# Cross attention and routed experts on one core: expert rows read as quarters and turned in 32x32 squares on VectorE, residual rows fetched by plain transfers

## What is computed

```python
x = x + attention(layernorm(x), ctx, ctx)      # 16 heads of 32, masks, Wq Wk Wv Wo
idx = argmax(position_table @ sign(tile_sigs)) # one expert of 8 for each of the 256 positions
x = x + layernorm(x) @ W[idx].T + b[idx]       # the same position in every batch has the same expert
```

## Time and profile before

| | us |
|---|---|
| median of three runs | 952.63 (950.90 to 953.97) |
| the profiled execution, its whole time | 953.35 |
| its span, first to last instruction | 951.4 |
| outside the span | 1.95 |

### The profile page before, as it was taken

One profiled execution on the slowest core, in us unless ns is written; L12 is line 12 of the kernel. 1 busy time (PEld: TensorE's weight loads), 2 busy tenths in 40 slices (PEclk: granted clock), 3 DMA queues, 4 the chain that ended last, 5 costly groups with the idle time before them and its releaser, 6 DMA issues.

```text
span 951.4 us, 16646 instructions
## 1 busy us (share of the span) xinstructions
PE 908.4 (95%) x5696; PEld 729.2 (77%) x5697; DVE 735.2 (77%) x1097; ACT 383.9 (40%) x697; POOL 567.1 (60%) x763
## 2 busy tenths in 40 slices
PE   5899999999999999999999999999739999999997
PEld 4687887887888788788878878887627888888885
DVE  5988867777776877877787787779758777777775
ACT  5554444454544445454444545444451111111110
POOL 3855746465574646557464654743645777777773
PEclk9999999999999999999999999999878999999999
DMA  9613133131313314131331313113643544444551
GB/s 336 225 72 102 56 113 91 60 121 46 104 53 113 101 53 117 45 110 48 113 102 56 113 45 113 52 51 117 224 142 112 158 161 162 163 158 159 162 164 50
DMA packets 48876, 108.10 MB, mean 114 GB/s; under 512 B 10496, under 2 KB 15136, under 8 KB 46624
## 3 DMA queue, kind: packets, MB, share of 16 engines
q1 hardware_dynamic: 37216, 71.70, 23.7%
q0 software_dynamic: 11200, 35.21, 11.6%
q10 hardware_dynamic: 384, 0.21, 0.1%
HBM read 73.47 MB, written 35.19 MB: 114 GB/s over the span
## 4 chain that ended last, share of the span: by engine, by line
PE 91%; DVE 3%; POOL 2%; DMA 1%; issue 1%; ACT 0%; SPq 0%; DVEq 0%; POOLq 0%
PE pS L1358 27%; PE pA L1652 21%; PE pA L1358 20%; PE pS L1416 7%; PE pA L1439 7%; PE pT L1427 6%; PE pT L1632 3%; PE pS L1384 1%; DMA x_scratch<-y 1%; POOL xt_lo L982 1%; POOL wo_lo L1030 0%; DMA wk_raw<-in_wk 0%; DMA xg<-x_scratch,gather_rows 0%; PE pT L1463 0%; DVE early L1312 0%
## 5 line engine op out<-in xcount | busy, mean ns | idle before, releaser
L1652 PE MATMUL pA<-wf_hl,x_hi 128*128 x560 | 183.3, 409 | 1.9 <-DVE x_lo L1586 1.9
L1203 DVE TENSOR_TENSOR s<-pS,bias 128x1024 f32<-128x1024 f32 x64 | 78.0, 1219 | 100.3 <-PE pS L1416 100.3
L998 POOL COPY y<-y_mom 128x1 f32<-128x1 f32 x64 | 12.9, 202 | 238.5 <-DVE y_mom L1242 238.5
L1015 POOL TENSOR_TENSOR s<-s,row 128x1024 f32<-128x1024 f32 x64 | 122.0, 1906 | 11.5 <-DVE row L1223 11.5
L1119 ACT CAST ot_hi<-pA 128x512 fp32r<-128x512 f32 x64 | 37.6, 588 | 222.6 <-PE pA L1439 222.6
L1546 POOL DMA_INDIRECT out_dram<-y,scatter_rows x70 | 94.1, 1344 | 54.4 <-DVE y L1594 52.8
L1565 ACT CAST x_hi<-pT 128x512 fp32r<-128x512 f32 x70 | 41.1, 587 | 191.0 <-PE pT L1632 159.1
L1652 PEld LDWEIGHTS pA<-wf_hl,x_hi 128*128 128x128 f32 x560 | 101.1, 191 | 21.2 <-issue 2.3
L1358 PE MATMUL pA<-wo_hi,ot_hi 128*128 128x512 f32 x256 | 109.2, 426 | 4.5 <-DVE ot_lo L1227 4.5
L1652 PE MATMUL pA<-wf_hl,x_lo 128*128 x280 | 111.5, 398 | 0.0
L1358 PE MATMUL pS<-xt_hi,wq_hi 128*128 128x512 f32 x256 | 105.6, 413 | 3.9 <-DVE wq_lo L1262 2.3
(11 more groups left out here) (124 smaller groups left out, 1898.9 us busy)
## 6 DMA issues: line engine op xcount, KB each, us to landing
x_scratch<-y SPq DMA_DIRECT2D x64, 257.0 KB, 3.0
xt_raw<-in_x_t SPq DMA_DIRECT2D x16, 1024.0 KB, 6.2
x<-in_x SPq DMA_DIRECT2D x64, 256.0 KB, 2.6
wf_hl<-in_wf SPq DMA_DIRECT2D x8, 1024.0 KB, 8.8
ctx_raw<-in_ctx_t SPq DMA_DIRECT2D x32, 128.0 KB, 3.1
bias_all<-in_bf SPq DMA_DIRECT2D x1, 2048.0 KB, 10.8
mask_early<-in_mask SPq DMA_DIRECT2D x1, 1536.0 KB, 11.6
xg<-x_scratch,gather_rows POOLq DMA_INDIRECT x70
```

What stands on the lines that cost most here:

```text
L1015: pool.tensor_tensor(p, p, h.row[:, t % h.c, 3, :].unsqueeze(2).broadcast_to([P, H, BK]), ALU.mult)\
L1203: dve.tensor_tensor(h.s_sb[:, t % h.c, :].rearrange("p (h k) -> p h k", h=H), pS[:, 0, :].rearrange("p (h k) -> p h k", h=H), h.bias[:, t ...
L1652: mm = pe.matmul(pA[:, r % 2, :], a[:, c * P:(c + 1) * P], w, start=(c == 0 and m == 0), stop=(c == KC - 1 and m == 2))
```

## The change

- In the attention stage each tile now leaves two things in DRAM: the normalised row (`y_normal`, made by ACT, `y_normalise`) in `x_quarters`, where a row is cut into four quarters of 128 floats that lie 32 x 256 rows apart; and the row with its expert's bias added (`y_biased`, made by POOL, `add_bias`) in `y_rows`. SP stores both (`store_rows`), and waits for both engines.
- The 2 MB broadcast of biases goes. In its place POOL gathers two sets of 128 bias rows by position in the prologue (`bias_at`), in front of its low part of Wo.
- In the expert stage the gathers go from POOL to SP and ACT as plain DMAs whose address comes from a register: for each block SP issues 4 (one for each position: 128 pieces of 512 bytes, `gather_quarters`) and ACT issues 4 (32 rows of 2048 bytes, `gather`). In front of each stands a `value_load` of the position from `gather_rows`.
- With quarters on the partitions, a VectorE transpose in squares of 32x32 gives the operand of the product, so PE's transposes go, DVE's `normalise` and `add_bias` go, and a DVE `transpose` comes. The rows of the expert matrices are reordered on the host to match.
- ACT's `high` and DVE's `low` read SBUF (`x2t`) and not PSUM. ACT issues the gathers of four blocks ahead of high(0), and then high(j), gather(j+4).
- POOL only scatters in the expert stage.

```diff
 def store_y(t):
-    sp.wait_ge(y_ready, t + 1)
-    sp.dma_start(x1[t * P:(t + 1) * P, :], h.y_sb[:, t % 2, :]).then_inc(y_stored[t % 2], 16)
+    sp.wait_ge(y_biased_ready, t + 1)
+    sp.wait_ge(y_normal_ready, t + 1)
+    store_rows(sp, slice(t * P, (t + 1) * P), t // 2, t % 2, t % 2)
...
+def store_rows(sp, rows, batch, half, ring):
+    sp.dma_start(y_rows[rows, :], y_biased[:, ring, :]).then_inc(y_stored[ring], 16)
+    dst = x_quarters.rearrange("(i b) s f -> b s i f", i=KC)
+    sp.dma_start(dst[batch, half * P:(half + 1) * P], ...
+                 y_normal[:, ring, :].rearrange("p (i f) -> p i f", i=KC)).then_inc(y_stored[ring], 16)
...
             rstd(0)
             rstd(1)
+            pool.wait_ge(rv, MATCHED + 1)
+            for n in range(2):
+                pool.indirect_dma_start(bias_at[:, n, :], None, bf,
+                                        bass.IndirectOffsetOnAxis(ap=expert_at[:, n:n + 1], axis=0)).then_inc(bias_loaded, 16)
             pool.wait_ge(w_hi_ready["o"], 1)
...
+            def add_bias(t):
+                wait(pool, y_stored[t % 2], 32 * (t // 2))
+                pool.tensor_tensor(y_biased[:, t % 2, :], y_sb[:, t % 2, 0:DM], bias_at[:, t % 2, :], ALU.add)\
+                    .then_inc(y_biased_ready, 1)
...
+            def y_normalise(t):
+                y = y_sb[:, t % 2, :]
+                act.wait_ge(y_ready, t + 1)
+                wait(act, y_stored[t % 2], 32 * (t // 2))
+                act.activation(y_normal[:, t % 2, :], y[:, 0:DM], ACT.Identity, bias=y[:, DM:DM + 1],
+                               scale=y[:, DM + 1:DM + 2]).then_inc(y_normal_ready, 1)
...
-                for t in (4, 5, 6, 7, 3):
+                y_normalise(h.tiles - 2)
+                expert_high(act, 4)
+                y_normalise(h.tiles - 1)
+                for t in (5, 6, 7, 3):
                     expert_high(act, t)
...
+        def experts_sync(sp):
+            def gather_quarters(j):
+                r = j % R
+                wait(sp, x2t_ready, j + 1 - R)
+                for n in range(PB):
+                    s = sp.value_load(gather_rows[n * B:n * B + 1, j:j + 1], min_val=0, max_val=S - 1)
+                    sp.dma_start(xq[:, r, n * P:(n + 1) * P],
+                                 x_quarters[:, bass.ds(s, 1), :].rearrange("p a f -> p (a f)")).then_inc(quartered[r], 16)
+            for j in range(NR):
+                gather_quarters(j)
...
+        def experts_scalar(act):
+            def high(j):
+                act.wait_ge(x2t_ready, j + 1)
+                wait(act, f_done, j - 1)
+                act.copy(x2_hi[:, j % 2, :], x2t[:, j % 2, :]).then_inc(x2_hi_ready, 1)
+            def gather(j):
+                r = j % R
+                wait(act, y2_ready, j + 1 - R)
+                for n in range(PB):
+                    s = act.value_load(gather_rows[n * B:n * B + 1, j:j + 1], min_val=0, max_val=S - 1)
+                    act.dma_start(yg[n * B:(n + 1) * B, r, :],
+                                  y_rows.rearrange("(b s) d -> b s d", s=S)[:, bass.ds(s, 1), :].rearrange("b a d -> b (a d)"))\
+                        .then_inc(gathered[r], 16)
             for b in range(2):
+                act.wait_ge(y_stored[b], 32 * SHORT.tiles // 2)
+            for j in range(R - 2):
+                gather(j)
             for j in range(NR):
                 high(j)
+                if j + R - 2 < NR:
+                    gather(j + R - 2)
...
-                dve.tensor_scalar(xn2[:, j % 2, :], xg[:, r, 0:DM], xg[:, r, DM:DM + 1], xg[:, r, DM + 1:DM + 2],
-                                  ALU.subtract, ALU.mult).then_inc(xn2_ready, 1)
+                dve.transpose(x2t[:, j % 2, :].rearrange("p (c g b) -> p c g b", c=KC, g=PB),
+                              xq[:, r, :].rearrange("p (g c a) -> p c g a", g=PB, c=KC)).then_inc(x2t_ready, 1)
...
-                for c in range(KC):
-                    mm = pe.transpose(pT[:, r % 2, c * P:(c + 1) * P], xn2[:, r % 2, c * P:(c + 1) * P], ident[:])
-                mm.then_inc(x2t_done, 1)
```

More of the change, by code:

```diff
@@ L282, in kernel_program @@
         wf_loaded = [sem(f"wf_loaded_{t}") for t in range(NE)]
-        wf_hi_ready = [sem(f"wf_hi_ready_{t}") for t in range(NE)]
+        wf_hi_ready = sem("wf_hi_ready")
+        HIGH_ORDER = (0, 1, 2, 4, 5, 6, 7, 3)
         wf_lo_pool = sem("wf_lo_pool")
@@ L1050, in tiles @@
                         xt_low(g + 2)
+                    if t == 2:
+                        pool.wait_ge(bias_loaded, 32)
+                    if t >= 2:
+                        add_bias(t - 2)
                     if t == h.tiles - 2:
@@ L1057, in tiles @@
                 y_rstd(h.tiles - 2)
+                add_bias(h.tiles - 2)
                 y_rstd(h.tiles - 1)
+                add_bias(h.tiles - 1)
             return tiles
@@ L1531, in kernel_program @@
         y2_ready = sem("y2_ready")
-        scattered = [sem(f"scattered_{r}") for r in range(R)]
+        scattered = [sem(f"scattered_{r}") for r in range(3)]
+        def experts_sync(sp):
[8 more added lines that the diff above has]
+                gather_quarters(j)
         def experts_gpsimd(pool):
             last_row = pool.to_reg(B * S - 1)
[L1537 to L1541, removed]
-                    .then_inc(gathered[r], 16)
             def scatter(j):
@@ L1547, in scatter @@
                                         y2[:, j % 3, :], None, bounds_check=last_row, oob_is_err=False)\
-                    .then_inc(scattered[j % R], 16)
+                    .then_inc(scattered[j % 3], 16)
+            for j in range(NR):
+                scatter(j)
+            for r in range(3):
+                pool.wait_ge(scattered[r], 16 * len(range(r, NR, 3)))
+        def experts_scalar(act):
[11 more added lines that the diff above has]
+                        .then_inc(gathered[r], 16)
@@ L1561, in experts_scalar, with transpose @@
-        def experts_scalar(act):
-            def high(j):
-                act.wait_ge(x2t_done, j + 1)
-                wait(act, f_done, j - 1)
-                act.copy(x2_hi[:, j % 2, :], pT[:, j % 2, :]).then_inc(x2_hi_ready, 1)
-            for j in range(NR):
                 high(j)
+                if j + R - 2 < NR:
+                    gather(j + R - 2)
         def experts_vector(dve):
-            def add_bias(j):
-                e = dve.value_load(expert_of[0:1, j:j + 1], min_val=0, max_val=NE - 1)
-                dve.tensor_tensor(xb[:, j % 2, :], xg[:, j % R, 0:DM],
-                                  bias_all[:, bass.ds(e, 1), :].rearrange("p a n -> p (a n)"), ALU.add)\
-                    .then_inc(xb_ready, 1)
-            def normalise(j):
+            def transpose(j):
@@ L1601, in experts_vector @@
             expert_low(dve, 5)
-            normalise(0)
-            normalise(1)
+            transpose(0)
+            transpose(1)
             expert_low(dve, 6)
             low(0)
-            add_bias(0)
             for j in range(NR):
@@ L1610, in experts_vector @@
                 if j + 2 < NR:
-                    normalise(j + 2)
+                    transpose(j + 2)
                 if j == 0:
@@ L1656, in body @@
             def body(k, n):
-                first = isinstance(k, int) and R * k + n == 0
-                if first:
-                    transpose(k, n + 1)
-                if is_block(k, n):
-                    e = expert(k, n)
-                if is_block(k, n + 1) and not first:
-                    transpose(k, n + 1)
-                if is_block(k, n):
-                    product(k, n, e)
-            turns = (NR - 5 - 1) // R
-            for n in range(-1, R):
+                product(k, n, expert(k, n))
+            turns = NR // R
+            for n in range(R):
                 body(0, n)
@@ L1672, in experts_tensor @@
                     body(k, n)
-            for n in range(NR + 1 - R * turns):
+            for n in range(NR - R * turns):
                 body(turns, n)
```

125 lines of the change are left out of this document (63 added, 62 removed).

## The result

The changed kernel takes 1086.55 us (median; 1084.05 to 1088.74), the kernel before 952.98 in the same comparison: a ratio of 1.140, 95% interval 1.137 to 1.144. The forecast was 1060 with a range of 985 to 1125.

What follows compares the result with a forecast made beforehand. PE was taken to bound the kernel before, the SP and ACT queues the changed expert stage. Attention and change-over to 711.3 us, gathers ahead, blocks at 4.7 us and the tail summed to 739.35 + 280 p, about 1060 us; range 985 to 1125.

Steps and rivals of the forecast that it cites:

- start of the first gather on ACT: Change-over: last attention store landed at 711.3 us, with 2.8 us from the prologue and 1.7 us from addition and second store.
- 16 pieces to the start of high(0): Start of expert stage: ACT issues gathers four blocks ahead, 16 p, plus 1.4 us for high, low and PE's start.
- high(0) to high(69): Expert stage: 66 blocks at 4.7 us, set by four pieces per queue, then three at 2.8 us without gathers in front.
- high(69) to the end, and outside the span: End of kernel: 2.8 us for the last product, 6.9 from last finish to end, 1.95 outside the span.
- The price of a piece: SP and ACT queues, expert stage: register load, checks, address and issue one after another, 1.15 us, between 0.98 and 1.49.
- The prologue: POOL's chain before wo_lo: two bias gathers of 1.4 us each with gap add 2.8 us, bounded by 0 and 3.1.
- The attention stage and the change-over: Attention adds nearly nothing, as PE bounds; at its end POOL's addition and second store issue add 1.7 us before landing.
- DVE's transpose: Expert stage: taken as 0.7 us, from 0.55 to 2.28; the skill's 128x128 figure gave 1.24; not the bound.
- Issue is cheap: Rival, expert stage: most of a piece hidden, PE bounds at 2.80 us a block, 924 us in all; chance 0.10.
- p: Expert stage: queue time for one gathered piece, 1.15 us; the sum is 739.35 + 280 p, break-even at 0.76.
- The transfers are the bound: Rival, expert stage: DMA packets take 3.1 us a block, at the upper end 5.4 and 1108 us; chance 0.12.
- PE's clock falls: Rival, expert stage: PE 60% busy drops to 1.2 GHz, 5.5 us a block, about 1114 us; chance 0.12.

Runs made afterwards that it cites:

- experiment 1: Changed kernel with constant positions for the gathers on both SP and ACT, so no register loads (real positions left out): 937.95 us.
- experiment 2: Changed kernel with constant positions on SP alone, ACT keeping its register loads: 1076.37 us.
- experiment 3: Changed kernel with constant positions on ACT alone, SP keeping its register loads: 1090.82 us.
- experiment 10: Changed kernel with one register load per block in each queue for all four pieces (three of four positions left out): 943.76 us.
- experiment 12: Changed kernel, complete, with four positions side by side read by one register load, no range checks, bias gathers late: 932.8 us, ratio 0.979 to the kernel before.
- experiment 4: Changed kernel, complete, with the two bias gathers moved from in front of wo_lo to the end of POOL's prologue: 1081.19 us.
- experiment 11: Changed kernel with rows written in block order by POOL, so gathers have fixed addresses; complete for these inputs: 1189.25 us, ratio 1.247 to the kernel before.
- experiment 5: Changed kernel with y rows gathered by one indirect POOL transfer, SP and ACT issuing two quarters each: 970.07 us, ratio 1.017 to the kernel before.
- experiment 6: As experiment 5, with the bias gathers at the end of POOL's prologue: 962.75 us, ratio 1.009 to the kernel before.
- experiment 7: As experiment 6, with six y2 buffers in place of three: 960.27 us, ratio 1.008 to the kernel before.
- experiment 8: As experiment 7, with POOL's scatter ahead of its gather: 962.28 us, ratio 1.010 to the kernel before.
- experiment 9: As experiment 7, with constant positions for the quarters (real positions left out): 953.25 us.

## Why the prediction was right, and by how much it was off

The mechanism and its place were right: a plain DMA with a computed address costs its queue more than a microsecond, two queues with four of them for a block are both above PE's time, and PE starves (experiments 1 to 3, 10 and 12). The forecast of 1060 was 2.4% low. Rebuilt with the times of the profiled execution (1088.74 us), the sum closes:

| term | predicted | measured | difference |
|---|---|---|---|
| start of the first gather on ACT | 711.3 | 722.09 | +10.8 |
| 16 pieces to the start of high(0) | 18.4 | 17.7 | -0.7 |
| high(0) to high(69) | 66 x 4.7 + 3 x 2.8 = 318.6 | 333.0 | +14.4 |
| high(69) to the end, and outside the span | 13.05 | 15.9 | +2.9 |
| sum | 1061.35 | 1088.7 | +27.4 |

**The price of a piece** (1.15 us) is the first term that was mis-sized, and for SP only. ACT's pace held: 4.67 us a block where 4.7 was forecast. SP pays 1.247 us on average: its register load has a median of 0.447 and goes up to 1.1 us, where I took PE's 0.30 of the earlier trace rows and not ACT's single 0.467, which was the nearer row. Checks (0.152 and 0.018) and issue (0.34) were as read. ACT, in its first 16 pieces, paid 17.7 / 16 = 1.11. Of the +14.4 us, 7.7 come from the 20 blocks after 956.91 us that still have a gather on ACT (101.7 us, not 94.0). Another 5.8 come from the last three blocks, forecast at 2.8 us each because ACT has no gather in front of them: they took 14.2 us, because SP's loads for them go on to 1069.6 us. The forecast cost the two queues as one and left SP out at the end. The first 46 blocks give the other +0.9. Of the +2.9 behind high(69), 2.5 lie between the last finish (1077.50 us) and the end, 9.4 us where the earlier trace rows has 6.9; what makes them is open.

The Trainium skill ("DMA: Bandwidth & Descriptors", section on issuing engines) calls the sequencer's time usually small relative to the DMA; here four pieces take 5.0 us of SP's queue beside a transfer load that needs at most 2.72 us a block (experiment 1), so the measurement stands against it for pieces of this size.

**The prologue** (+2.8 us) was the second. PE's q projection starts at 52.26, and not at 44.99 as in the earlier trace rows: +7.3 us. The two gathers were sized about right (1.20 and 0.95 us, with gaps 2.5 in all); what I didn't see is the DVE pass beside them (experiment 4), because I costed the gathers on POOL's own list alone. That is 4.5 of the +10.8 us at the first gather.

**The attention stage and the change-over** make the rest of the +10.8. POOL's timeline there, and SP's; then a piece of the chain and ACT's timeline:

```profile
709.27 1.27 POOL L1019 TENSOR_TENSOR y_biased<-y,bias_at 128x512 f32<-128x512 f32 x1
...
711.80 1.09 POOL L1019 TENSOR_TENSOR y_biased<-y,bias_at 128x512 f32<-128x512 f32 x1
```

```profile
710.95 1.75 SPq L419 DMA_DIRECT2D x_scratch<-y_normal  x1
...
713.95 0.44 SPq L419 DMA_DIRECT2D x_scratch<-y_normal  x1
```

```profile
712.75 6.72 DMA wf_hl<-in_wf
```

```profile
719.49 1.90 ACT L302 CAST wf_hl<-wf_hl 128x2048 fp32r<-128x2048 f32 x1 [1.41 <-DMA wf_hl<-in_wf]
```

The last residual is computed at 707.37, before at 697.24: 7.3 us of that from the prologue. The other 2.8 come in the attention stage and not in its last tiles: the residuals are 7.3 us later at tile 0, 9.3 at tile 20 and 10.1 at tile 40 and at the last. That is no more than the runs of the kernel before differ among themselves (950.90 to 953.97), so whether the change makes it is open. From there to the last store go 6.6 us, before 2.8: +3.8 and not +1.7, because two additions stand one behind the other on POOL (tile 62's holds up tile 63's statistics) and SP takes 1.75 us for one issue whose median over 64 tiles is 0.435. From the last store to the first gather go 8.1 us, where the forecast leaves 6.75 (711.3 less 700.05 + 2.8 + 1.7). The forecast let ACT wait for the stores alone. By its list ACT also makes the high part of the last expert matrix first, whose load SP issues between the last two tiles' stores; that copy ended at 721.39. The stores landed hardly earlier, as SP, which waits for them alone, had its first load at 721.7; so either would have held the start.

**Held as forecast:** the attention stage stays full with POOL at 68.5 and ACT at 56.0 of 100 us, so 64 additions and 64 passes cost 2.8 us there at most. DVE's transpose takes 0.70 to 0.71 us, the value taken, and not the 1.24 of the estimate beside it. PE's wait for low is 1.5 to 1.6 us a block near 800 us (1.9 forecast). DMA share 0.52 to 0.55 and not 0.65, as the block is longer. First product near 741 and not 731, by the terms above.

**Rivals.** *Issue is cheap*: refuted; p is 1.25 on SP, the break-even was 0.76. Its sum for a block of 2.8 us, 924, is near what experiments 1 and 12 reach with no load or one load in place of four. *The transfers are the bound*: refuted by experiments 1 and 12, though its estimate of 3.1 us a block was high: 2.72 us carries them at a DMA share of 0.94. *PE's clock falls*: it did fall at the change-over (0.50 in 720 to 740 us, the lower of the two levels, with PE idle) and was 0.88 to 0.98 in the stage, but PE stood idle waiting for x_lo 55 times there, so it was not the bound; and with the loads gone PE was full at a clock of 1.00.

## What to carry to other kernels

Count the instructions of a queue as you count those of an engine: a DMA with an address from a register is a load, a check, address arithmetic and an issue, here 1.1 to 1.25 us, and the busy columns show none of it. If plain transfers are to take the place of an indirect one, lay the positions side by side and load them with one instruction; that, with the range checks left out and the bias gathers late (some 5 us), turned 14% slower into 2% faster. Cost each queue by itself, to its last instruction: two queues of nearly the same price take turns as the bound. And price an instruction that is put on one engine by what runs on its neighbours at that moment too: two short gathers on POOL cost 7.3 us at PE's start, not 2.8.

## What the runs showed of the hardware

- A register load of four neighbouring elements had a median of 0.325 us (ACT) and 0.493 us (SP), one of a single element 0.452 and 0.447; the single ones on ACT come as 0.28 and 0.47 us in turn.
- One DVE pass over 128x1024 floats took 2.99 to 3.27 us in eight traces, where a long POOL pass had begun over 2 us ahead of it, and 10.67 to 10.77 us in six, where the POOL passes began just after it.
- A 32x32-square transpose of 128x512 floats took 0.70 us on DVE.
- With 512-byte pieces at two steps out of 4 KB rows, the DMA engines were busy for 35% of the time and moved 122 GB/s, while the stage waited for them; with quarters at one regular step the stage moved 285 GB/s (experiments 11 and 1).
- In experiments 5 to 9 the signal of a finished product reached the two engines that wait for it some 2.2 to 2.8 us late, once in three or four blocks; why is open.
